# A recurrent mixer with experts: the next group's front moved among the scan steps, and the skip term partly on VectorE

## The reference

```
proj = layernorm(x) @ W_in.T                  # z (256), xc (256), dt_raw (4), bc (2048)
u    = silu(conv4(xc) + bias)                 # 4 heads of 64
dt   = clip(softplus(dt_raw + dt_bias), 1e-4, 0.1)
B, C = l2norm(bc[..., 0, :]), l2norm(bc[..., 1, :])   # 4 heads, two halves y and v of 128 states
# A = (pi sigmoid(theta))^2, kdamp = 0.5 sigmoid(k), for each token:
denom = 1 + dt kdamp + dt^2 A
v = (v - dt A y + dt u Bv) / denom
y = y + dt v + dt u By
o = y . Cy + v . Cv
out = ((o + skip * u) * silu(z)) @ W_out.T
```

## Time and profile before

| | us |
|---|---|
| median of 3 runs | 531.29 (530.99 to 531.33) |
| the profiled execution | 531.18 |
| its span, first to last instruction | 529.4 |

### The profile page before, as it was taken

How to read it: one execution, slowest core, us unless ns; L and a number is a source line. 1 busy time by engine, 2 the same in 40 slices (tenths; PEclk the granted TensorE clock), 3 DMA queues, 4 the chain that set the end, 5 groups by cost and what they waited for, 6 DMA issues and landing times.

```text
span 529.4 us, 9508 instructions
## 1 busy us (share of the span) xinstructions
PE 446.4 (84%) x3185; PEld 344.8 (65%) x3185; DVE 445.4 (84%) x1268; ACT 242.6 (46%) x482; POOL 282.7 (53%) x367
## 2 busy tenths in 40 slices
PE   6980159996989989997889969898789969998997
PEld 5360158774756667675757659676656658876986
DVE  7699988968999999968999998968889998787542
ACT  1522227443475436442575526443466534343463
POOL 2007887656108876657108686567305776777000
PEclk9686559999999979999999988999899998998999
DMA  7500000200000001200000000110000000000000
GB/s 221 169 1 0 1 1 2 81 2 1 0 1 1 1 1 43 80 2 2 1 0 2 0 2 21 47 36 2 1 0 2 1 1 22 1 2 1 1 11 11
DMA packets 14794, 10.23 MB, mean 19 GB/s; under 512 B 1797, under 2 KB 13966, under 8 KB 14618
## 3 DMA queue, kind: packets, MB, share of 16 engines
q1 hardware_dynamic: 14746, 9.63, 6.2%
HBM read 8.55 MB, written 1.07 MB: 18 GB/s over the span
## 4 chain that ended last, share of the span: by engine, by line
DVE 41%; PE 37%; POOL 9%; issue 8%; ACT 3%; DMA 1%; SPq 0%; DVEq 0%; POOLq 0%; ACTq 0%
PE BC L612 6%; DVE tpA L1291 6%; DVE GV L1291 5%; DVE xr L1439 5%; PE HB L515 4%; DVE BC L1302 4%; PE GV L634 4%; POOL vt L1628 3%; PE HB L572 3%; PE HB L504 3%; POOL rinv L1663 2%; DVE mm L1339 2%; DVE GV L1302 2%; PE HB L622 2%; PE OO L693 2%
## 5 line engine op out<-in xcount | busy, mean ns | idle before, releaser
L612 PE MATMUL BC<-xnT,winT 128*128 128x128 f32 x512 | 78.8, 303 | 40.7 <-ACT pr L926 22.8
L612 PEld LDWEIGHTS BC<-xnT,winT 128*128 128x128 f32 x512 | 69.3, 211 | 54.1 <-issue 28.9
L1625 POOL TENSOR_TENSOR big<-mm 128x256 f32<-128x256 f32 x64 | 50.2, 784 | 52.3 <-DVE mm L1339 45.7
L1648 POOL TENSOR_SCALAR uT<-uT,skipT 128x512 f32<-128x512 f32 x8 | 12.5, 1570 | 89.3 <-DVE w L1424 53.9
L564 PE MATMUL HB<-xnT,w 128*128 128x512 f32 x108 | 52.0, 603 | 3.7 <-ACT gtm L1013 2.1
L1628 POOL TENSOR_TENSOR vt<-mm 128x256 f32<-128x256 f32 x64 | 53.9, 842 | 0.0
L634 PE MATMUL GV<-big,vt 128*128 128x128 f32 x256 | 44.0, 296 | 8.9 <-POOL vt L1628 8.9
L1637 POOL TENSOR_TENSOR mm<-ab,pr 128x256 f32<-128x256 f32 x48 | 41.4, 884 | 14.9 <-ACT pr L926 14.9
L950 ACT ACTIVATE big<-GV 128x256 f32<-128x256 f32 x60 | 23.1, 384 | 56.8 <-PE GV L637 55.5
L1337 DVE TENSOR_TENSOR mm<-BC,pr 128x512 f32<-128x512 f32 x64 | 44.2, 691 | 5.7
L634 PEld LDWEIGHTS GV<-big,vt 128*128 128x128 f32 x256 | 35.4, 200 | 16.8 <-POOL vt L1628 13.6
(11 more groups left out here) (212 smaller groups left out, 1117.1 us busy)
## 6 DMA issues: line engine op xcount, KB each, us to landing
ab<-dt_rows SPq DMA_DIRECT2D x12, 256.0 KB, 4.2
xr<-in_x SPq DMA_DIRECT2D x4, 256.0 KB, 4.9
winT<-in_w_inT SPq DMA_DIRECT2D x1, 1024.0 KB, 6.5
w<-in_rw SPq DMA_DIRECT2D x1, 1024.0 KB
out<-xr SPq DMA_DIRECT2D x3, 256.0 KB, 3.0
taps<-in_dw_wT SPq DMA_DIRECT2D x1, 512.0 KB, 3.8
w<-in_sw SPq DMA_DIRECT2D x2, 128.0 KB
out<-xr SPq DMA_DIRECT2D x2, 128.0 KB, 1.8
```

The costliest lines, as they stand in the source:

```text
L612: last = pe.matmul(b[:, j * TS:(j + 1) * TS], winT[:, col:col + NS], xt, start=True, stop=True)
L1625: pool.tensor_tensor(wt[q % 8][:], m[:, 0], m[:, 3], ALU.add)
```

## The change

**The front of group g + 1 is taken out of the pair loop of group g.** On VectorE the new `front_stage(g + 1, slot)` is called from `between`, behind the router and the experts, in the steps of group g: statistics in slots 0 to 3, aggregates in 4 and 5, epsilon in 6, the logits' bias in 32 and minimum in 34, and the twelve instructions of the chain in slots 52 to 63, one in each. An instruction waits for its predecessor (`behind`) only when it is itself due, where `link` waited at once. On the other engines the work of group g + 2 stands in the expert loop of group g, which runs beside the steps of group g + 1: normalizing after expert 2, transposes after 3, logits after 4, the exponential (with its table load) after the sixth conversion, n = 5. Group 1's is put among the conversions of group 0. GpSimd's `scale_and_shift` goes ahead of the skip gate (in group 0 behind it). The transposes of dt and the copy to `rows8` stand ahead of the pair loop. The order of the shared banks follows.

**Denominators** come at k = 0, 1, 2 and 4. The running sums stay at 16 and 17.

**The skip term.** For the first three tiles of a group `tile_out` adds `uT` to `y1` in a second VectorE instruction, and `op` has two matmuls in place of four. The fourth tile is done as before.

```diff
+F_DENS, DENS_AT = (9, 10, 12, 13), (0, 1, 2, 4)
+SCANS_AT = (16, 17)
+S_STATS, S_AGGR, S_EPS, S_LOGITS, S_DT = 0, 4, 6, 32, 52
+XN_AFTER, XNT_AFTER, LOGITS_AFTER = 2, 3, 4
+DT_OPS = 12
...
             # TensorE, op
-                pe.wait_ge(skip_done, g + 1)
                 pe.wait_ge(y1_done, tile + 1)
-                for i in range(2):
-                    pe.matmul(OO[:, 2 * TS:2 * TS + DM], uT[:, i, c * TS:(c + 1) * TS], woT[:, i, :],
-                              start=(i == 0), stop=False)
+                if c == GT - 1:
+                    pe.wait_ge(skip_done, g + 1)
+                    for i in range(2):
+                        pe.matmul(OO[:, 2 * TS:2 * TS + DM], uT[:, i, c * TS:(c + 1) * TS], woT[:, i, :],
+                                  start=(i == 0), stop=False)
...
             # TensorE, ahead of group 0's first projections, and ahead of each pair loop
+            norm_T(LN1, 1)
+            logits(1)
...
+                if g + 1 < NG:
+                    rows_of_dt(g + 1)
...
             # TensorE, pair loop
-                        front_early(g + 1, k)
+                        if k in DENS_AT:
+                            denominator(g + 1, DENS_AT.index(k))
...
             # TensorE, expert loop, behind hidden(g, e)
+                        if g + 2 < NG:
+                            if e == XNT_AFTER:
+                                norm_T(LN1, g + 2)
+                            if e == LOGITS_AFTER:
+                                logits(g + 2)
...
             # ScalarE, group 0's conversions
                 convert(0, n)
+                if n == 0:
+                    norm1(1)
+                if n == 1:
+                    xnT_copy(1)
+                if n == 2:
+                    logits_copy(1)
+                if n == 4:
+                    step_exp(1)
...
             # ScalarE, expert loop
                                 convert(g + 1, n)
+                                if n == 5 and g + 2 < NG:
+                                    step_exp(g + 2)
+                        if g + 2 < NG:
+                            if e == XN_AFTER:
+                                norm1(g + 2)
+                            if e == XNT_AFTER:
+                                xnT_copy(g + 2)
+                            if e == LOGITS_AFTER:
+                                logits_copy(g + 2)
...
             # VectorE, front_stage(g, slot): the chain
+                n = slot - S_DT
+                if n == 0:
+                    dve.wait_ge(dt_exp, g + 1)
+                    chained(dve.tensor_scalar(le, le, E_MAX, None, ALU.min))
+                if n == 1:
+                    behind()
+                    chained(dve.tensor_scalar(lp[0], le, 1.0 / 9, None, ALU.mult))
+                if 2 <= n < DT_OPS - 2:
+                    i, m = n - 2, 10 - n
+                    behind()
+                    chained(dve.scalar_tensor_tensor(out=lp[(i + 1) % 2], in0=lp[i % 2],
+                                                     scalar=(1.0 if m % 2 else -1.0) / m, in1=le,
+                                                     op0=ALU.add, op1=ALU.mult))
...
             # VectorE, tile_out
+                if c < GT - 1:
+                    dve.wait_ge(skip_done, g + 1)
+                    dve.wait_ge(y_part, (GT - 1) * g + c + 1)
+                    dve.tensor_tensor(y, y, uT[:, :, c * TS:(c + 1) * TS], ALU.add).then_inc(y1_done, 1)
...
             # VectorE, between
+                if g + 1 < NG and slot < 2 * DS:
+                    front_stage(g + 1, slot)
...
             # GpSimd, fills
-                skip_gate(g)
+                if g == 0:
+                    skip_gate(g)
+                if g + 1 < NG:
+                    scale_and_shift(ln_index(LN1, g + 1))
+                if g:
+                    skip_gate(g)
```

More of the change, by code:

```diff
@@ L350, in build @@
                 plan(what, 0, i)
+        plan("xnT", 1)
+        plan("logits", 1)
         for g in range(NG):
+            if g + 1 < NG:
+                plan("rows", g + 1)
             for k in range(STEPS_OF[g]):
@@ L477, in norm_T, with logits @@
                 last.then_inc(h_ready, 1)
-            def front_early(g, k):
+            def logits(g):
+                pe.wait_ge(h_free, h_read_of("xnT", g))
+                hb = h_bank("logits", g)
+                for c in range(GT):
+                    last = pe.matmul(hb[:, NH * c:NH * c + NH],
+                                     xnTs[g % 2][:, HALO + c * TS:HALO + (c + 1) * TS],
+                                     winT[:, COL_DT:COL_DT + NH], start=True, stop=True)
+                last.then_inc(h_ready, 1)
@@ new lines, in rows_of_dt, with denominator @@
+            def rows_of_dt(g):
+                pe.wait_ge(dt_done, g + 1)
+                hb = h_bank("rows", g)
+                for c in range(GT):
+                    last = pe.transpose(hb[0:2 * NH, c * TS:(c + 1) * TS],
+                                        dtts[g % 2][:, c].rearrange("p i h -> p (i h)"), ident[:])
+                last.then_inc(h_ready, 1)
+            def denominator(g, h):
+                pe.wait_ge(h_free, h_read_of("rows", g))
+                hb = h_bank("den", g, h)
+                pe.matmul(hb[:], coef8[:, h, :], rows8, start=True, stop=True).then_inc(h_ready, 1)
@@ L480, in front_early, with front_first @@
+            def front_first(k):
                 if k == F_XNT:
-                    norm_T(LN1, g)
+                    norm_T(LN1, 0)
                 if k == F_LOGITS:
[L484 to L489, removed]
@@ L490, in front_early @@
-                    last.then_inc(h_ready, 1)
-                if k == F_ROWS:
[L493 to L504, removed]
+                    logits(0)
@@ L1145, in front_early, with running_sum @@
+            def running_sum(g, f):
+                dve.wait_ge(h_free, h_read_of("den", g, NH - 1))
+                run = view(lden, KP * MID if f else KP * MID - 1, (1 if f else -1, KP * MID))
+                dve.tensor_tensor_scan(run, keep[:], run, 0.0, ALU.mult, ALU.add if f else ALU.subtract)\
+                    .then_inc(lcum, 1)
             def front_early(g, k):
@@ L1147, in front_early @@
                     norm_stats(LN1, g)
-                if g == 0 and k == F_XN:
+                if k == F_XN:
                     norm_apply(LN1, g)
```

166 lines of the change are left out of this document (110 added, 56 removed).

## The result

The changed kernel takes 549.9 us (median of 6 runs, 548.58 to 552.46) against 531.31 us for the kernel before beside it: ratio 1.033, 95% interval 1.028 to 1.038. The direction was forecast, the size was not: 535.6 us, with a range that ended at 541. The profiled execution took 550.33 us, its span is 548.6 us (before: 529.4), and the mean granted clock of TensorE is 0.903 (before: 0.932). Executions over 1.5% above the fastest of their kernel count as slow and are left out of every ratio, and the profiles of e2 (550.93 us), e15 (548.70) and e18 (595.32, at a granted clock of 0.73 throughout) are of such executions.

What follows compares the result with a forecast made beforehand. VectorE and TensorE, each 84% busy, were taken to bound the kernel by stage. 531.2 us, steps +16.1, first halves -10.4, second halves -1.8, rest +0.5: 535.6 us; own range 532.5 to 539, whole range 525 to 541.

Steps and rivals of the forecast that it cites:

- the steps: VectorE's 32 steps per group, taking in the next group's front: 4.3 us in group 0, 5.9 in groups 1 and 2.
- first halves: Pairs 0 to 8 of groups 0 to 2: 74.6 us become 64.2, a gain of 10.4 (4.8 to 17.3).
- second halves: Pairs 8 to 15 of groups 0 to 2: 25.1 us instead of 25.7, -1.8 in all (bounds -3.8 and +1).
- the rest: Third tile's addition behind pair 15 and group 3's pair loop, gaining on TensorE what it pays on VectorE: +0.5 us.
- I get pair 8 at 21.4 us behind pair 0 in every group: First eight pairs: four denominators add 1.05 us to TensorE three times, VectorE's savings absorb part; bounds 19.1 and 23.3.
- Rival 3: Exponential later still (2.7 us or more), low clock meets denominators, each first half 22.5 us: 542.1 us; chance 0.1.
- The exponential's wait: Slot 52 in the steps of groups 1 and 2 stalls for ScalarE's exponential: 2.0 us each, between 1.1 and 2.7.
- The lock: All-SBUF VectorE chain instructions in slots 52 to 63 each wait for GpSimd's running fill: +2.8 us in group 0.
- The statistics: Four VectorE instructions in the first step slots, 0.2 us each: 0.3 us in group 0, 0.8 in groups 1 and 2.
- The first (no lock): In the steps, the lock doesn't bind 16-element instructions behind the strided fills: 526.4 us; chance 0.15.
- The second (the pairs give back all): VectorE sets the pairs' pace, so they return all it drops, 19.2 us, first half 20.0: 529.6 us; chance 0.2.

Runs made afterwards that it cites:

- e2: Changed kernel with the clamped exponential of the step sizes kept in a PSUM bank; median 548.27 us, ratio 1.020 from its first two executions.
- e15: Changed kernel with 24 idle transposes on TensorE after each group's first denominator, where TensorE waits for the first products; 545.85 us, ratio 1.023.
- e18: e9 with 24 idle transposes on TensorE at the head of the pairs; 523.62 us, ratio 0.981.
- e6: Changed kernel with clamped exponential in PSUM, exponential one conversion earlier and denominators late, at steps 9, 10, 12, 13; 535.59 us, ratio 1.006.
- e4: Changed kernel with the exponential of groups 2 and 3 one conversion earlier on ScalarE, for one more table load; 543.56 us, ratio 1.020.
- e3: Changed kernel with the denominators back at steps 9, 10, 12 and 13 of the pair loop; 547.88 us.
- e16: e3 with the transposes and the copy of the step-size rows also back in the pair loop, at step 8; 545.7 us.
- e17: Changed kernel with one ScalarE logarithm replacing the polynomial, denominators and step-size rows back in the pair loop, no skip split; 532.63 us, ratio 0.999.
- e9: Kernel before with one ScalarE logarithm replacing the ten polynomial instructions of the step sizes; 524.85 us, ratio 0.985.
- e14: Changed kernel without the skip split; 553.56 us, ratio 1.039.
- e12: Changed kernel with the step-size chain three slots earlier, starting at slot 49; executed once, 557.94 us.
- e10: e9 with the skip split in groups 0 to 2 and not in the last group; 524.93 us, ratio 0.987.

## Why the prediction was wrong

It gave the steps +16.1 us, first halves -10.4, second halves -1.8 and the rest +0.5, together +4.4; the span grew by 19.2. By the table the 14.8 us between are: first halves 5.2, steps 3.8, the prologue 2.1, second halves of groups 0 to 2 2.0, behind pair 15 of these groups 1.3, group 3 0.4.

**The step that failed** is "I get pair 8 at 21.4 us behind pair 0 in every group". It came to 22.7, 22.2 and 24.5. The denominators were priced at 1.05 us each from rows at full clock, and the projections were taken to be just in time. But the head of the pairs ran at 1.2 GHz for a good part. In group 0 the clock had been low since the steps (46.2 us); in groups 1 and 2 TensorE waited 1.32 and 3.04 us for the first products, and the clock was low from 210.1 and 332.9 on. Three of the twelve denominators took 2.07 us, and a pair's projections 2.08 (1.16 at full clock). e15 shows the price: 9.8 us over three groups, more than the 5.2 that the halves missed by. At full clock, e15's halves less what the transposes hold up, they would have been some 18.5, 20.5 and 20.5 us (an estimate), under the forecast. TensorE carries 66 to 76% of the chain in the changed kernel's halves, and 16 to 25% in e6's, with late denominators. Rival 3 named this ("the low clock meets the denominators") with a later exponential, at 0.1 and 542.1 us; it was nearest, and still 8 us short.

**Steps.** The mechanism was right and its size off. The exponential's wait was 3.24 and 3.27 us, not 2.0 and beyond the bound of 2.7; e4 shows its worth. The lock was priced "one for one", 2.8 us in group 0. It came to 2.5 in e3's trace, and to 5.4 at one instruction in the changed kernel's (5.61 less its own length of 0.17). In groups 1 and 2 chain instructions took 1.6 us over their own length, against 1.9 forecast for the lock there. Missing altogether was the rows copy before the first squares (1.06 us in group 1; e3, e16). The statistics start their successors 0.2 us later, as forecast, and cost groups 1 and 2 1.0 us.

**Second halves.** -1.8 was forecast, +0.2 measured. They lost TensorE work (23.61 busy us in group 0, before 25.48) and did not shorten. e17 against e9 shows one side: what the first half gains, the second gives back when the denominators stand there. What holds the changed kernel's own second half at 25.4 us, with TensorE idle 2.8 of 26.4 in group 0, no run tested; e14 shows only that it is not the split. The forecast had it held by TensorE and VectorE. In the chain that ended last TensorE fell from 72 to 79% of these halves to 37 to 42%, and GpSimd, which the sum left out, rose from 14% to 38 to 40%.

**Not in the sum.** Behind pair 15 the clock falls with the split in 36 of 36 cases, against 3 of 12. That this comes of the 0.4 us less that TensorE has to do there (6.92 against 7.33 in 9.2) is argued, not shown. The prologue's code is unchanged, and its +2.1 us is not the change's in full: in seven variants of the changed kernel with the polynomial (e2, e3, e4, e12, e14, e15, e16) and in e6 VectorE reached the first step between 39.2 and 42.0 us. e9 and e10 differ too, with one prologue: 36.7 and 38.4. Why it varies was not tried.

**Rivals 1 and 2.** The first (no lock) is refuted by e2 and e12. The second (the pairs give back all) was right on the first half alone, and only with late denominators: 17.4 to 19.8 us in e3, under its 20.0.

## What to carry to other kernels

A small VectorE instruction between SBUF operands is not small beside an unbroken stream of GpSimd's: give it one operand in PSUM, or replace the chain by an instruction elsewhere, as the logarithm did (-1.5% alone). Price matmuls that move to the head of a stage at the clock that the rows there show, and the work around them too. Work moved out of a stage that two engines bound in turn moves the wait to the other one: measure the loop as a whole, since the second half gave back 7.1 of the 12.7 us that the first half gained in e3.

## What the runs showed of the hardware

- A VectorE instruction from SBUF to SBUF took 5.61 and 6.96 us beside unbroken GpSimd instructions, two of them in 1.5 to 1.7 us, and ended with the last; in another run it slipped in behind one of them (0.53). With a PSUM operand it took 0.17.
- TensorE's granted clock fell from 1.00 to 0.50 at 138.4 us of the changed kernel, behind 9.2 us with 6.92 of work, and stood at 1.00 again from 145.2.
- Transposes put into a wait of TensorE gave the work behind them the full clock (7.33 us for 8.97 to 11.52), and held it up by 1.3 to 3.2 us where they outlasted the wait.
- The logarithm of 1 + e with its wait costs ScalarE 0.25 us for 16 elements of each partition; ten VectorE instructions did the same.
